# Split expert weights: once per expert and copied per tile by transfers, instead of split per tile on VectorE

## The reference, cut to what matters

```python
x = x + _L0_gnn_ref(_layernorm(x), adj, ...)   # 5 node groups, two graph convolutions each
x = x + _L0_ffn_ref(_layernorm(x), ...)        # 8 experts 128->512->128, top 2 of 8
x = x + _L1_gnn_ref(_layernorm(x), adj, ...)   # one graph convolution
x = x + _L1_ffn_ref(_layernorm(x), ...)        # shared MLP and 4 small experts, top 2
```

```python
gate_scores = jnp.einsum('bsd,ed->bse', x, Wg) + bg
topk_scores, topk_idx = jax.lax.top_k(gate_scores, K)
combine = sum over k of softmax(topk_scores)[k] * one_hot(topk_idx[k], E)
for e in range(E):
    h = jax.nn.relu(jnp.einsum('bsd,hd->bsh', x, W1[e]) + b1[e])
    y = jnp.einsum('bsh,dh->bsd', h, W2[e]) + b2[e]
    out = out + combine[..., e:e + 1] * y
```

## Time and profile before

| | |
|---|---|
| runs | 1250.98, 1252.68, 1254.02 us; median 1252.68 |
| profiled execution | 1253.57 us, span 1251.8 us, mean granted TensorE clock 0.938 |
| PE | 1143.5 us busy, 91% of the span |
| DVE | 1060.6 us, 85% |
| ACT | 949.8 us, 76% |
| POOL | 735.5 us, 59% |
| DMA | 124.51 MB, mean 99 GB/s |

### The profile page before, as it was taken

How to read it: one execution, slowest core, us unless ns; L and a number is a source line. 1 busy time by engine, 2 the same in 40 slices (tenths; PEclk the granted TensorE clock), 3 DMA queues, 4 the chain that set the end, 5 groups by cost and what they waited for, 6 DMA issues and landing times. The chain is left out here.

```text
span 1251.8 us, 20777 instructions
## 1 busy us (share of the span) xinstructions
PE 1143.5 (91%) x6346; PEld 856.7 (68%) x6346; DVE 1060.6 (85%) x3170; ACT 949.8 (76%) x1885; POOL 735.5 (59%) x678
## 2 busy tenths in 40 slices
PE   6889979459999999999999981899999999999998
PEld 4667756327788888888888861566667666666675
DVE  4678987897999999999999975688888888888875
ACT  3448765448999999999999971687787877877874
POOL 3346555636666666655666617776677766777720
PEclk9999985559999999999999995899999999999999
DMA  5579764502323333322333542223222232222310
GB/s 196 195 221 293 228 196 143 200 21 74 83 81 76 84 83 85 83 78 79 83 85 85 72 64 70 58 76 85 69 72 73 70 88 72 70 73 72 81 37 26
DMA packets 136466, 124.51 MB, mean 99 GB/s; under 512 B 14591, under 2 KB 116067, under 8 KB 135204
## 3 DMA queue, kind: packets, MB, share of 16 engines
q1 hardware_dynamic: 119075, 87.77, 22.8%
q0 software_dynamic: 17280, 35.42, 13.2%
HBM read 83.64 MB, written 39.50 MB: 98 GB/s over the span
## 5 line engine op out<-in xcount | busy, mean ns | idle before, releaser
L1081 POOL DMA_INDIRECT exg<-xln_scratch,ids x284 | 279.5, 984 | 190.9 <-PE p_ex L1134 105.4
L1380 POOL DMA_INDIRECT yg<-expert_rows_scratch,pos_i x256 | 254.5, 994 | 97.1 <-issue 72.7
L1102 ACT ACTIVATE ehr<-p_eh,bc 128x512 f32<-128x512 f32 x284 | 195.2, 687 | 22.7 <-DVE ehl L1222 19.2
L1222 DVE TENSOR_TENSOR ehl<-ehr,ehh 128x512 fp32r<-128x512 f32 x284 | 191.4, 691 | 7.0 <-ACT ehh L1105 6.8
L1105 ACT ACTIVATE ehh<-ehr 128x512 fp32r<-128x512 f32 x284 | 179.6, 633 | 9.0
L1138 PE MATMUL p_eh<-exh,wh 128*128 128x512 f32 x284 | 124.6, 439 | 0.8 <-ACT exh L1096 0.8
L1150 PE MATMUL p_ey<-ehl,wh 128*128 128x512 f32 x284 | 116.8, 411 | 0.0
L1387 POOL TENSOR_TENSOR root_l<-pre_l,mhalf 128x4 f32<-128x4 f32 x64 | 66.5, 1039 | 80.1 <-DVE pre_l L1654 79.2
L1142 PE MATMUL p_eh<-exl,wh 128*128 128x512 f32 x284 | 112.1, 395 | 0.0
L1139 PE MATMUL p_eh<-exh,wl 128*128 128x512 f32 x284 | 112.0, 394 | 0.0
L1147 PE MATMUL p_ey<-ehh,wh 128*128 128x512 f32 x284 | 112.0, 394 | 0.1
(11 more groups left out here) (226 smaller groups left out, 2912.4 us busy)
## 6 DMA issues: line engine op xcount, KB each, us to landing
expert_rows_scratch<-eyo SPq DMA_DIRECT2D x71, 256.0 KB, 2.3
xtok<-in_x_tok SPq DMA_DIRECT2D x8, 1024.0 KB, 7.3
an<-in_a_t SPq DMA_DIRECT2D x16, 512.0 KB, 4.7
xln_scratch<-xl SPq DMA_DIRECT2D x16, 512.0 KB, 4.4
at<-in_a_t SPq DMA_DIRECT2D x32, 256.0 KB, 3.0
out<-outx SPq DMA_DIRECT2D x32, 256.0 KB, 2.6
wj<-in_w_grp SPq DMA_DIRECT2D x16, 321.0 KB, 4.8
exg<-xln_scratch,ids POOLq DMA_INDIRECT x284, 2.6
```

Of the source, the lines that this page charges most:

```text
L1081: pool.indirect_dma_start(out=xg[p][:, k, :], out_offset=None, in_=xln_d, in_offset=bass.IndirectOffsetOnAxis(ap=ids[:, R * j + k:R * j + ...
L1102: nc.scalar.activation(hr[c % 2][:, :], p_h[c][:, :], ACT.Relu, bias=bc[p][:, c:c + 1])\
L1222: nc.vector.tensor_tensor(hl[:, c, :], hr[c % 2][:, :], hh[:, c, :].bitcast(F32), ALU.subtract)\
L1380: pool.indirect_dma_start(out=yg[p][:, c, k, :], out_offset=None, in_=y_d, in_offset=bass.IndirectOffsetOnAxis(ap=pos_i[:, c, R * j + k:R ...
```

## The change

Each expert's 1024 columns of weights are split once. In turns 2 to 9 of the first stage SP loads one expert's part of `wall` per turn; in turns 3 to 10 ScalarE casts it to `whi`, in turns 4 to 11 VectorE subtracts, and the low part `wlo` takes the place of the weights in `wall`. In the expert stage SP reads the tile's expert number and copies the two halves of `whi` and `wlo` into `wh` and `wl` by four transfers of 256 KB from on-chip memory to on-chip memory; for tile j+2 as soon as tile j has made its last hidden chunk and its last `down`. VectorE only copies the six bias columns (`biases`), and it takes over `turned` from ScalarE, between h_lo(j, 2) and h_lo(j, 3). The thirteen constants of the last stage are loaded in the expert stage by SP, behind the store of tile 1.

To make room for `whi` (32 KB per partition) `ar` and `orl` go: the adjacency is loaded straight into `ag` (now five buffers), the identity is added in place, the relu is done in place in `os` (so VectorE waits for the store before it writes `os` again). The masks of the router are 16-bit, `deg_sums` is half as wide and added to in two steps, unused columns of `cf` are gone, the constants' tiles are allocated after the second stage, and the last stage's `he` lies on `whi`. The rest of the diff follows from this.

```diff
-GA = 4
+GA = 5
...
+        whi = alloc(top, "whi", [P, E0, WW], F32R)
+        wlo = wall[:, :, 0:WW].bitcast(F32R)
         lc_loaded = sem("l_consts_loaded")
         NC = 13
...
-        mask = [alloc(lgp, f"mask{k}", [P, B, E0]) for k in range(2)]
+        mask = [alloc(lgp, f"mask{k}", [P, B, E0], F16) for k in range(2)]
         mb = alloc(lgp, "mb", [P, B, E0], F16)
-        dsum = alloc(lgp, "deg_sums", [P, 2 * R, N])
+        dsum = alloc(lgp, "deg_sums", [P, R, N])
...
-        w_loaded = sem("w_loaded")
+        w_loaded = [sem(f"w_loaded{k}") for k in range(4)]
+        whi_ready = sem("w_high_ready")
+        wlo_ready = sem("w_low_ready")
+        W0 = 2
...
                         sp.dma_start(xg[j % 2][:, :, :], x_grp[item[j]]).then_inc(loaded[j % 2], 16)
-                        sp.dma_start(ar[j % 2][:, :, :], a_grp[item[j]]).then_inc(loaded[j % 2], 16)
+                        if j >= GA:
+                            sp.wait_ge(o_done, j - GA + 1)
+                        sp.dma_start(ag[j % GA][:, :, :], a_grp[item[j]]).then_inc(loaded[j % 2], 16)
...
-                        sp.dma_start(dst, orl[j % 2][0:rows, :, :]).then_inc(rows_stored[j % 2], 16)
+                        sp.dma_start(dst, os_[j % 2][0:rows, :, :]).then_inc(rows_stored[j % 2], 16)
...
+                        if W0 <= t < W0 + E0:
+                            sp.dma_start(wall[:, t - W0, :], w_exp[:, t - W0, :]).then_inc(w_loaded[(t - W0) % 4], 16)
...
-                        if j >= GA:
-                            pool.wait_ge(o_done, j - GA + 1)
-                        nc.gpsimd.tensor_tensor(ag[j % GA][:, :, :], ar[j % 2][:, :, :], plus, ALU.add)\
+                        nc.gpsimd.tensor_tensor(ag[j % GA][:, :, :], ag[j % GA][:, :, :], plus, ALU.add)\
...
-                        pool.wait_ge(deg_ready, b + 1)
-                        nc.gpsimd.tensor_tensor(dsum[:, :, :], dsum[:, :, :], an[b % 2][:, :, :], ALU.add)\
-                          .then_inc(deg_ready, 1)
+                        for h in range(2):
+                            pool.wait_ge(deg_ready, 2 * b + h + 1)
+                            nc.gpsimd.tensor_tensor(dsum[:, :, :], dsum[:, :, :], an[b % 2][:, h * R:h * R + R, :],
+                                                    ALU.add).then_inc(deg_ready, 1)
...
+                        if W0 < t <= W0 + E0:
+                            e = t - W0 - 1
+                            act.wait_ge(w_loaded[e % 4], 16 * (e // 4) + 16)
+                            nc.scalar.activation(whi[:, e, :], wall[:, e, 0:WW], ACT.Copy).then_inc(whi_ready, 1)
...
-                            act.wait_ge(rows_stored[p], 16 * (t // 2) - 15)
-                            nc.scalar.activation(orl[p][:, :, :], os_[p][:, :, :], ACT.Relu).then_inc(orl_ready, 1)
+                            nc.scalar.activation(os_[p][:, :, :], os_[p][:, :, :], ACT.Relu).then_inc(orl_ready, 1)
...
+                        if W0 + 1 < t <= W0 + 1 + E0:
+                            e = t - W0 - 2
+                            dve.wait_ge(whi_ready, e + 1)
+                            nc.vector.tensor_tensor(wlo[:, e, :], wall[:, e, 0:WW], whi[:, e, :].bitcast(F32),
+                                                    ALU.subtract).then_inc(wlo_ready, 1)
...
                             dve.wait_ge(b2_s, t - 1)
+                            dve.wait_ge(rows_stored[p], 16 * (t // 2) - 15)
...
-                @block.sync
-                def _(sp):
-                    sp.dma_start(wall[:, :, :], w_exp).then_inc(w_loaded, 16)
-                    for dst, src in ((wgcn[:, :], w_gcn), (bgcn[:, :], b_gcn), (maskt[:, :], mask_t),
-                                     (ws[:, :], w_s), (bs[:, :], b_s), (w1[:, :, :], e_w1), (w2[:, :, :], e_w2),
-                                     (w3[:, :, :], e_w3), (be[:, :], b_e), (vraw[:, :, :], b_out),
-                                     (gws[:, :], gw), (gbs[:, :], gb), (selraw[:, :, :, :], selp_d)):
-                        sp.dma_start(dst, src).then_inc(lc_loaded, 16)
-                    sp.wait_ge(w_loaded, 16)
-                    sp.wait_ge(lc_loaded, 16 * NC)
...
+                    rows = y_d.rearrange("(t p) d -> p t d", p=P)
+
+                    def l_constants():
+                        for dst, src in ((wgcn[:, :], w_gcn), (bgcn[:, :], b_gcn), (maskt[:, :], mask_t),
+                                         (ws[:, :], w_s), (bs[:, :], b_s), (w1[:, :, :], e_w1), (w2[:, :, :], e_w2),
+                                         (w3[:, :, :], e_w3), (be[:, :], b_e), (vraw[:, :, :], b_out),
+                                         (gws[:, :], gw), (gbs[:, :], gb), (selraw[:, :, :, :], selp_d)):
+                            sp.dma_start(dst, src).then_inc(lc_loaded, 16)
+
+                    def weights(j, e, half, copied):
+                        cols = slice(half * H0, (half + 1) * H0)
+                        for dst, src in ((wh, whi), (wl, wlo)):
+                            sp.dma_start(dst[j % 2][:, cols].bitcast(F32),
+                                         src[:, bass.ds(e, 1), cols].rearrange("p a w -> p (a w)").bitcast(F32))\
+                              .then_inc(copied[j % 2], 16)
+
+                    def of_tile(j):
+                        return sp.value_load(texp[0:1, bass.ds(j, 1)], min_val=0, max_val=E0 - 1)
+
+                    sp.wait_ge(set_, 1)
+                    for j in range(2):
+                        e = of_tile(j)
+                        weights(j, e, 0, w1_copied)
+                        weights(j, e, 1, w2_copied)
                     for j in range(NTP):
                         p = j % 2
+                        if j + 2 < NTP:
+                            e = of_tile(j + 2)
+                            sp.wait_ge(h_done, HC * j + HC)
+                            weights(j + 2, e, 0, w1_copied)
+                            sp.wait_ge(y_done, j + 1)
+                            weights(j + 2, e, 1, w2_copied)
                         sp.wait_ge(yo_ready, j + 1)
-                        sp.dma_start(dst[:, j * R:j * R + R, :], yo[p][:, :, :]).then_inc(stored[p], 16)
+                        sp.dma_start(rows[:, j * R:j * R + R, :], yo[p][:, :, :]).then_inc(stored[p], 16)
+                        if j == 1:
+                            l_constants()
                     for p in range(2):
                         sp.wait_ge(stored[p], 16 * ((NTP + 1 - p) // 2) + 1)
+                    sp.wait_ge(lc_loaded, 16 * NC)
...
-                    def turned(j, i, p):
-                        act.wait_ge(yo_done, j + 1)
-                        act.wait_ge(stored[p], 8 * i + 1)
-                        nc.scalar.activation(yo[p][:, :, :], p_yo[:, :, :], ACT.Copy).then_inc(yo_ready, 1)
-
-                    def turn(i, p, after, before):
+                    def turn(i, p, after):
                         j = i + p
                         hidden(j, p, 0)
                         hidden(j, p, 1)
                         if after:
                             evacuate(j + 1, 1 - p)
                         hidden(j, p, 2)
-                        if before:
-                            turned(j - 1, i if p else i - 2, 1 - p)
                         hidden(j, p, 3)
 
                     evacuate(0, 0)
                     for j in range(NTP):
-                        turn(j - j % 2, j % 2, j < NTP - 1, j >= 1)
-                    last = NTP - 1
-                    turned(last, last - last % 2, last % 2)
+                        act.wait_ge(bc_ready, j + 1)
+                        turn(j - j % 2, j % 2, j < NTP - 1)
...
-                        pe.wait_ge(w1_ready, j + 1)
+                        pe.wait_ge(w1_copied[p], 32 * (j // 2) + 32)
...
-                        pe.wait_ge(w2_ready, j + 1)
+                        pe.wait_ge(w2_copied[p], 32 * (j // 2) + 32)
...
-                    def take(j, p, w, half, ready):
-                        cols = slice(half * H0, (half + 1) * H0)
-                        nc.vector.tensor_copy(wh[p][:, cols], w[:, cols]).then_inc(wh_ready, 1)
-                        dve.wait_ge(wh_ready, 2 * j + half + 1)
-                        nc.vector.tensor_tensor(wl[p][:, cols], w[:, cols], wh[p][:, cols].bitcast(F32),
-                                                ALU.subtract).then_inc(ready, 1)
-
                     def of_tile(j):
-                        e = dve.value_load(texp[0:1, bass.ds(j, 1)], min_val=0, max_val=E0 - 1)
-                        return wall[:, bass.ds(e, 1), :].rearrange("p a w -> p (a w)")
-
-                    def take_1(j, p, w):
-                        nc.vector.tensor_copy(bc[p][:, :], w[:, WW:EW])
-                        take(j, p, w, 0, w1_ready)
+                        return dve.value_load(texp[0:1, bass.ds(j, 1)], min_val=0, max_val=E0 - 1)
+
+                    def biases(p, e):
+                        nc.vector.tensor_copy(bc[p][:, :], wall[:, bass.ds(e, 1), WW:EW]
```

(60 more changed lines are left out.)

21 lines of the change are left out of this document (7 added, 14 removed).

## The result

The changed kernel takes 1280.41 us (median of 4 runs, 1276.85 to 1282.02), the kernel before beside it 1253.35 (1250.98 to 1255.49): ratio 1.0211, 95% interval 1.0196 to 1.0227. It is slower by 27 us where 16 were forecast, inside the forecast range of 1256 to 1291 us. On a second chip, in a later comparison, the two took 1274.79 and 1252.21: ratio 1.0175 (1.0151 to 1.0200).

A forecast was written before the change was run, and what follows sets the result against it. TensorE was taken to bound the expert stage, a closed chain through VectorE and TensorE the first stage. First stage 7, constants 11, clock 2.2, VectorE's relief -4.1 gave +16 us: median 1269 us, range 1256 to 1291.

The forecast's parts named there:

- VectorE's relief: Expert stage: with VectorE's work cut, TensorE's wait on ehl goes; 68 tiles gain 0.06 us each, -4.1 us.
- The constants: Expert stage, turn 4: weights wait behind thirteen constants, with vraw on one DMA engine; +11 us, once.
- clock: Expert stage, after the stall at turn 4: TensorE runs 4.4 us at half speed, costing +2.2 us.
- The first stage: First stage, turns 4 to 11: VectorE's subtraction delays dinv, 1.2 us per plain turn; +7 us, bounds 1 and 12.
- The low bound: Turn 4 of the expert stage: if vraw were spread over all engines, SP's order alone would cost 3.8 us.
- rival (c): First stage: TensorE's idle grows and the clock halves in 5 plain turns; 22 us, 1291; chance 0.12.
- The copies at no cost: Expert stage: 1.05 MB of weight copies per tile fit the DMA engines, share about 0.87; cost 0.
- latency fits: Expert stage: weight halves are requested 7.3 and 7.4 us ahead; two 256 KB transfers need about 4 us.
- The sum: Whole kernel: 7 + 11 + 2.2 - 4.1 = +16 us, median 1269; forecast's chance 0.58.
- (a): Small price: constants cost 4 us, no clock loss, subtraction +1; 1253 to 1258, taken 1256; chance 0.15.
- (b): Faster: tile 4's weights come in time and the subtraction hides beside ag; 1249.5; chance 0.08.
- (d): DMA-bound expert stage: on-chip copies occupy engines twice per byte, 5.5 us at least, 7.6 per tile; +81, 1350; chance 0.07.

The follow-up runs named there:

- the distinct rows: Changed kernel with filling entries and empty tiles at the end naming row p on partition p in place of row 0: 1290.66 us, ratio 1.0252.
- all four kernels that ran there: Changed kernel with one edit each: vraw cut, constants one per tile, distinct rows, subtraction behind zs; ratios 1.0226, 1.0277, 1.0252, 1.0258.
- the kernel before, one wait added: Kernel before, with GpSimd's first-stage addition waiting until VectorE has issued xsb of the same turn: 1248.56 us, ratio 0.9981.
- the changed kernel with five edits: Changed kernel with vraw cut, constants one per store, distinct rows, subtraction behind zs, and GpSimd's addition behind xsb: 1249.43 us, ratio 0.9980.

## Why the prediction was right and wrong, by its steps

- **VectorE's relief (forecast 4.1 us).** Right in its mechanism: L1150's wait is gone and a tile takes 6.40; without copies the stage is 5.0 us shorter than before. It is more than the 4.1 that I called the most, because the tile got 0.08 us shorter and not 0.06: I took the 6.42 of the last tile of the kernel before as the floor. That ScalarE's copy fits on VectorE at no cost was right too (0.68 us each).
- **The constants (forecast 11.0, clock 2.2).** The mechanism was right: one gap at turn 4, ended by a DMA into wl, share 0.07 in its tail, half clock behind it, and cutting vraw in 96 and 1 takes 8.4 to 9.4 us off. The size was near: 15.2 against 13.2, and 13.9 on the second chip. The wait is 12.5 us in place of 11, and TensorE then runs 5.2 us at a granted clock of 0.50 (331.57 to 336.79), 2.7 us of loss in place of 2.2. What was missing is that vraw holds SyncE as well: 1.59, 1.43 and 1.05 us for issues that I set at 0.47, so that the weights are issued 10.3 us behind the store, where my spacing gave 6.6. The low bound, a wait of 3.8 us without vraw's obstacle, was met once and missed once: with vraw cut tile 4 waits 3.87 us in one kernel and 5.40 in the other, and loses 5.7 and 7.05, half clock included.
- **The first stage (forecast 7, bounds 1 and 12).** 8.7 us at its end, 7.05 on the second chip. A plain turn got 0.89 us longer (9.03 in place of 8.14), not 1.2: wdi, not dinv, now waits beside the addition. Here is the changed kernel:

```profile
59.01 1.22 DVE L668 TENSOR_TENSOR wall<-wall,whi 128x1024 fp32r<-128x1024 f32 x1
...
59.45 1.90 POOL L399 TENSOR_TENSOR ag<-ag,cf 128x512 f32<-128x512 f32 x1
...
60.14 1.24 DVE L692 TENSOR_SCALAR wdi<-dinv,wb 128x4 f32<-128x4 f32 x1
...
62.74 1.21 PE L566 MATMUL p_z<-zs,ag 128*128 128x128 f32 x8 [2.15 <-DVE zs L710]
...
63.74 3.57 PE L575 MATMUL p_h<-yt,wj 128*128 128x512 f32 x4
```

  VectorE's 128x4 instruction runs from 60.14 to 61.38 and ends with GpSimd's addition (61.35): the exclusive pair that the earlier trace rows showed. In two of the turns the clock fell as well, as rival (c) had it: granted 0.50 from 63.72 to 67.13 us, p_h 3.57 us in place of 1.88, turns of 10.7. That is 1.7 us twice, not in five turns; TensorE had waited 2.15 us for zs, not 2.4. So the sum came near the forecast in part by luck, with one term smaller and one that I had given to a rival.
- **The copies at no cost.** This step failed, and with it "latency fits": 0 us were forecast, 10.1 came, and 6.0 on the second chip. The volume was right and even too high: share 0.76 to 0.78 at 245 to 254 GB/s, where I had 0.87. What I left out was who else is on those engines. A copy lands in 3.0 to 3.2 us at the median, but gathers of one row from the filling entries take what the share of 0.76 leaves (3.7 us in the last four tiles, shown by the distinct rows). The rest, tiles 7 and 30 above all, stays open as to its cause: these stalls are gone without the copies, and that loads of code come late there was only read from the queues. The page's landing times of the changed kernel:

```profile
wh<-whi SPq DMA_DIRECT2D x142, 256.0 KB, 3.0
wl<-wall SPq DMA_DIRECT2D x142, 256.0 KB, 3.2
expert_rows_scratch<-eyo SPq DMA_DIRECT2D x71, 256.0 KB, 2.7
```

  The store takes 2.7 us where the earlier trace rows had 2.3. The row that would have warned me was in the trace of before: share 1.00 at 77 GB/s in its last tiles. I read one window of the middle as the whole stage.
- **The sum.** 8.75 + 15.2 + 10.1 + 0.2 - 5.8 = 28.4 us for the two profiled spans (the last term is the shorter tile, what remains of the expert stage's 19.45), against 7 + 13.2 + 0 - 4.1 = 16. Most of the miss is the copies' term. Rivals (a), (b) and (d) did not happen: no tile was bound by the copies' volume. The 5.5 us that (d) starts from follow from no row: at the 304 GB/s of the forecast's own 3.45 us, twice the bytes would be 6.9.

What stays open: the 7.4 us at tile 1 on one chip, in all four kernels that ran there, what makes the stalls that the distinct rows leave, and how far they vary from run to run; one profile per kernel cannot tell.

## What to carry to other kernels

Before transfers are added to a stage, read its DMA share against its GB/s in every part of it, not in the middle only: where the share rose while the rate fell, the added transfers were late here. A transfer of 97 partitions was here a serial job at 25 GB/s, and it held the issuing queue too; cut the odd partition off before anything is moved around such a transfer. And when two engines shut each other out, look for a place where one of them waits for a third: the subtraction of 1.2 us was free there, and lengthened a turn by 0.89 us where it stood before.

The best versions are 1248.56 us (the kernel before, one wait added) and 1249.43 us (the changed kernel with five edits), both 0.2% under the kernel before.

## What the runs showed of the hardware that I had not expected

- While the transfer of 97 partitions drains at a DMA share of 0.07, its issuing queue is held: issues of 0.4 us take 1.05 to 1.59 us, and 2.15 and 3.08 us with copies of weights queued too. Cut in 96 and 1 it holds nothing (0.36 to 0.43 us).
- A tile's 512 reads of one row of 512 B fill the DMA engines (share 0.75 to 1.00 at 45 to 77 GB/s, the store among it), where the middle of the same stage, with distinct rows and the same stores, has a share of 0.33 at 82 GB/s.
- Transfers of 8 and 16 KB of a kind called instruction share the DMA engines with the data. Where one met a share of 0.92, TensorE and ScalarE stood for about 2 us together. That the transfer is the cause was not tested: most tiles that hold one are no longer than the others.
- The granted clock was 0.50 from 63.72 to 67.13 us in the first stage, behind a wait of TensorE of 2.15 us; behind the same wait one turn before (at 53.7 us) it stayed at 1.00.
